# Latent attention block: queries in ten products with packed weights, partner rows by DMA, the split on GpSimd, another order

## The reference, cut to what matters

```python
q_hk  = (hidden_q @ Wq.T).reshape(B, S, 16, 128)
q_big = einsum('bshk,hkq->bshq', q_hk, w_kc_q)            # 192 wide, per head
q_big = q_big * cos_q + rotate_half(q_big) * sin_q        # partner of element j is j +- 96
kv_r  = rope(kv_c)                                        # 1601 keys, 64 wide
q_r   = einsum('bshq,hqr->bhsr', q_big, W_qr)
k_r   = einsum('bld,hdr->bhlr', kv_r, W_kr)
attn  = softmax(einsum('bhsr,bhlr->bhsl', q_r, k_r))
ctx_c = einsum('bhsl,bld->bhsd', attn, kv_r)
out   = einsum('bhsd,hkd->bhsk', ctx_c, w_kc_kv) ... @ Wo.T
```

## Time and profile before

| what | value |
|---|---|
| median of 3 runs | 1802.81 us (1801.43 to 1810.01) |
| profiled execution: its own time | 1803.73 us |
| profiled execution: span of instructions | 1802.5 us |
| busy over the span: PE, PEld, DVE, ACT, POOL | 93%, 82%, 80%, 67%, 45% |
| mean granted PE clock | 0.97 |
| chain that ended last | PE 72%, DVE 14%, ACT 4%, issue 4%, DMA 3%, POOL 2% |

### The profile page before, as it was taken

One profiled execution on the slowest core, in us unless ns is written; L12 is line 12 of the kernel. 1 busy time (PEld: TensorE's weight loads), 2 busy tenths in 40 slices (PEclk: granted clock), 3 DMA queues, 4 the chain that ended last, 5 costly groups with the idle time before them and its releaser, 6 DMA issues.

```text
span 1802.5 us, 40836 instructions
## 1 busy us (share of the span) xinstructions
PE 1673.0 (93%) x14656; PEld 1470.0 (82%) x14656; DVE 1439.6 (80%) x3666; ACT 1200.3 (67%) x3004; POOL 810.2 (45%) x720
## 2 busy tenths in 40 slices
PE   7999998889999888899999999999999998888995
PEld 6999976658866666799999999999999997665884
DVE  5777757859856865799999999999999997786995
ACT  5766764326634543688888888888888985542663
POOL 5744422247854532444434443444444441224774
PEclk8999999879999998899999999999999999998997
DMA  5000019332339000000000000000000002402233
GB/s 176 25 1 1 1 56 362 96 99 44 52 65 280 9 2 2 23 13 13 13 12 13 30 13 13 13 13 13 13 13 1 2 2 96 197 2 86 45 52 73
DMA packets 51860, 91.61 MB, mean 51 GB/s; under 512 B 4592, under 2 KB 43632, under 8 KB 49232
## 3 DMA queue, kind: packets, MB, share of 16 engines
q1 hardware_dynamic: 42928, 78.16, 13.0%
q0 software_dynamic: 8160, 10.29, 3.6%
q10 hardware_dynamic: 576, 0.56, 0.1%
HBM read 56.13 MB, written 32.87 MB: 49 GB/s over the span
## 4 chain that ended last, share of the span: by engine, by line
PE 72%; DVE 14%; ACT 4%; issue 4%; DMA 3%; POOL 2%; SPq 0%; DVEq 0%; ACTq 0%; POOLq 0%
PE bank L100 59%; PE bank L2680 10%; DVE a_t L707 1%; DVE d_nm L1442 1%; PE bank L1938 1%; DVE a_t L704 1%; DVE d_nm L1441 1%; DMA g_sums<-g_y,g_xs 1%; DMA c_sums<-c_y,c_xs 1%; POOL c_rows L1803 1%; PE bank L1910 1%; PE bank L505 1%; PE bank L1175 1%; DVE d_lifted L1470 1%; DVE tiny L133 0%
## 5 line engine op out<-in xcount | busy, mean ns | idle before, releaser
L2780 ACT ACTIVATE e_P<-bank,e_st 128x496 f32<-128x496 f32 (+2 forms) x512 | 305.8, 599 | 32.9 <-DVE e_st L2862 32.9
L2858 DVE TENSOR_REDUCE e_st<-bank 128x1 f32<-128x496 f32 (+2 forms) x512 | 288.4, 571 | 33.7 <-PE bank L100 23.7
L2881 DVE TENSOR_TENSOR e_PT_lo<-bank,e_PT_hi 128x512 fp32r<-128x512 f32 (+1 forms) x448 | 280.9, 644 | 30.3 <-ACT e_PT_hi L2800 29.3
L2680 PE MATMUL bank<-ident,e_P 128*128 128x128 f32 (+1 forms) x1664 | 256.6, 273 | 4.0 <-DVE e_PT_lo L2881 3.9
L2800 ACT CAST e_PT_hi<-bank 128x512 fp32r<-128x512 f32 (+1 forms) x448 | 247.0, 553 | 17.7 <-PE bank L2680 10.2
L100 PE MATMUL bank<-e_PT_hi,e_kv 128*128 128x256 f32 (+1 forms) x832 | 232.1, 300 | 3.1 <-DVE e_cx_lo L2888 3.1
L100 PE MATMUL bank<-e_PT_lo,e_kv 128*128 128x256 f32 (+1 forms) x832 | 214.8, 279 | 0.0
L100 PE MATMUL bank<-e_KT,e_qk_hi 128*128 128x496 f32 (+2 forms) x512 | 207.1, 405 | 5.2 <-ACT e_P L2780 3.8
L2680 PEld LDWEIGHTS bank<-ident,e_P 128*128 128x128 f32 (+1 forms) x1664 | 197.2, 140 | 17.5 <-issue 3.1
L100 PE MATMUL bank<-e_KT,e_qk_lo 128*128 128x496 f32 (+2 forms) x512 | 177.3, 346 | 0.0
L100 PEld LDWEIGHTS bank<-e_PT_hi,e_kv 128*128 128x128 f32 (+1 forms) x832 | 156.9, 189 | 8.5 <-DVE e_cx_lo L2888 3.8
(11 more groups left out here) (493 smaller groups left out, 5281.1 us busy)
## 6 DMA issues: line engine op xcount, KB each, us to landing
c_wall<-in_c_w SPq DMA_DIRECT2D x8, 1536.0 KB, 18.9
g_wall<-in_g_w SPq DMA_DIRECT2D x8, 1536.0 KB, 19.3
c_rows<-normed SPq DMA_DIRECT2D x9, 1040.0 KB, 12.0
g_rows<-normed SPq DMA_DIRECT2D x9, 1040.0 KB, 13.5
e_stage<-in_e_w SPq DMA_DIRECT2D x16, 416.0 KB, 3.2
c_xs<-c_rows SPq DMA_DIRECT2D x23, 130.0 KB
g_xs<-g_rows SPq DMA_DIRECT2D x23, 130.0 KB
landing<-in_a_wo SPq DMA_DIRECT2D x2, 1024.0 KB, 6.1
```

The lines of the kernel that those rows point to most:

```text
L2680: last = pe.transpose(o[0:rows, c * SEQ + i * P:c * SEQ + (i + 1) * P], p[:, i, k0:k0 + rows], ident[:])
L2780: act.activation(Pm[u % 2][:, i, STARTS[j]:STARTS[j] + n], bank[score_bank[j]][:, 0:n], ACT.Exp, bias=s[:, i, 4:5], accum_out=s[:, i, j:j ...
L2858: last = dve.tensor_reduce(s[:, i, j:j + 1], bank[score_bank[j]][:, 0:PIECES[j]], AX.X, ALU.max)
L2881: dve.tensor_tensor(lo, bank[tb_bank[at % 2]][0:rows, 0:n * SEQ].rearrange("p (c n) -> p c n", c=n), hi.bitcast(F32), ALU.subtract).then_i ...
```

## The change

- `project_q`: the folded weights of a head stand in one tensor of 384 columns: upper parts of 128 query rows, upper parts of the other 64, lower parts of those 64, lower parts of the 128. The first 128 rows take 2 chunks x 3 products as before. The other 64 rows take 2 chunks x 2 products: upper and lower weights side by side are one stationary matrix of 128 columns, multiplied by the upper and by the lower input. That makes 10 products. The rows that come from lower weights are carried as rows of their own through the rotation, and `w2` has the rows of the 64 twice, so that absorption (still 6 products, now of 128 rows) sums them.
- Query elements are reordered in groups of 32 so that the partner of a row is 32 partitions away: `swap` brings the partner rows to `r2` with four DMAs of 32 partitions on SP's queue for each unit; all tensors of the rotation have 128 partitions.
- `split_z` on POOL rounds and subtracts (the rounding was ACT's `upper_z`); one multiplication of 512 takes the place of two of 256 in `rope_q`. The rotation of unit 1 is issued before the block starts, `r1` and `r2` of odd units lie in a tensor that was there already.
- `lower_q` is two DVE instructions in place of one.
- The order of the steps in the loops of PE, ACT and DVE is another, the fetch of a head's weights is issued behind the swap of a unit, and the prefetch of block f is issued by ACT at the middle of the loop.

The diff, cut to its core (eight columns of indentation taken off):

```diff
                 ahead.sync_early()
+                ahead.sync_last()
 ...
                     routing.weigh(1)
-                if ahead and i == N:
-                    ahead.upper_z(0)
 ...
         self.kvb = [A(f"kv{b}", [P, KT, P], F32R) for b in range(BATCH)]
-        self.ropeq = A("ropeq", [HALFQ, 4, SEQ])
+        self.ropeq = A("ropeq", [P, 4, SEQ])
 ...
-        self.r1, self.r2 = ([x_in[0:HALFQ, 2 * i:2 * i + 2, :]] for i in range(2))
-        self.r0 = [x_in[0:HALFQ, 2 * i:2 * i + 2, :] for i in (2, 3)]
+        self.r1, self.r2 = ([x_in[:, 2 * i:2 * i + 2, :]] for i in range(2))
+        self.r0 = [x_in[:, 2 * i:2 * i + 2, :] for i in (2, 3)]
         flat = rows32[:, 1:TILES, :].rearrange("p a n -> p (a n)")
         self.swapped = [flat[:, i * n_ctx:(i + 1) * n_ctx].rearrange("p (k d) -> p k d", k=KT) for i in range(2)]
+        for n, x in enumerate((self.r1, self.r2)):
+            x.append(flat[:, 512 * n:512 * (n + 1)].rearrange("p (c n) -> p c n", c=2))
         self.ropek = landing[:, 0:2 * n_ctx].rearrange("p (a k d) -> p a k d", a=2, k=KT)
 ...
         self.k_turned, self.k_kept, self.padded = S_("k_turned"), S_("k_kept"), S_("padded")
+        self.q_swapped = [signal(f"xs_in{i}") for i in range(2)]
         self.twice = Count(sem("pool_link"))
 ...
-        QW, HALFQ = self.QW, self.HALFQ
+        QW = self.QW
         self.stage.append(A("stage", [P, 832]))
-        self.stage_r.append(A("stage_r", [LAT, 320]))
-        self.wq.append([A(f"wq_{x}", [P, DC, QW], F32R) for x in ("hi", "lo")])
-        self.w2.append([A(f"w2_{x}", [HALFQ, 2, P], F32R) for x in ("hi", "lo")])
-        self.qr.append([A(f"qr_{x}", [HALFQ, 2, SEQ], F32R) for x in ("hi", "lo")])
+        self.stage_r.append(A("stage_r", [LAT, 3 * P]))
+        self.wq.append(A("wq", [P, DC, 2 * QW], F32R))
+        self.w2.append([A(f"w2_{x}", [P, 2, P], F32R) for x in ("hi", "lo")])
+        self.qr.append([A(f"qr_{x}", [P, 2, SEQ], F32R) for x in ("hi", "lo")])
 ...
         sp.dma_start(self.stage_r[h % 2][:], t["e_wr"][h]).then_inc(*self.w_in[h % 2].up(16))
+
+    def swap(self, m):
+
+        sp.wait_ge(*self.q_kept.at(m + 1))
+        for q in range(4):
+            at, to = 32 * q, 32 * (q ^ 1)
+            sp.dma_start(self.r2[m % 2][to:to + 32], self.r0[m % 2][at:at + 32]).then_inc(*self.q_swapped[m % 2].up(16))
 ...
             sp.dma_start(self.ctx_raw[b % 2], t["ctx"][b]).then_inc(*self.ctx_in[b - 2].up(16))
+
+    def sync_last(self):
+        sp.wait_ge(*self.x_roped.at(BATCH))
+        for m in range(2):
+            self.swap(m)
 ...
     def fold_r(self, h, o):
-        r, QW, HALFQ = self.stage_r[h % 2], self.QW, self.HALFQ
+        r = self.stage_r[h % 2]
         for c in range(2):
-            last = mm(o[0:HALFQ, c * P:(c + 1) * P], r[:, c * HALFQ:(c + 1) * HALFQ], r[:, QW:QW + P], True, True)
+            last = mm(o[:, c * P:(c + 1) * P], r[:, c * P:(c + 1) * P], r[:, 2 * P:3 * P], True, True)
         last.then_inc(*self.r_folded.up())
 ...
         h, b = divmod(m, BATCH)
-        w, HALFQ = self.wq[h % 2], self.HALFQ
+        w = self.wq[h % 2]
         if m < BATCH:
 ...
         pe.wait_ge(*self.wq_lo.at(h + 1))
-        for c in range(2):
-            for d in range(DC):
-                last = mm3(o[0:HALFQ, c * SEQ:(c + 1) * SEQ], [x[:, d, c * HALFQ:(c + 1) * HALFQ] for x in w],
-                           (XT_hi[:, d, tok(b)], XT_lo[:, d, tok(b)]), d == 0, d == DC - 1)
+        for d in range(DC):
+            mm3(o[:, 0:SEQ], (w[:, d, 0:P], w[:, d, 2 * P:3 * P]), (XT_hi[:, d, tok(b)], XT_lo[:, d, tok(b)]),
+                d == 0, d == DC - 1)
+        for d in range(DC):
+            for n, x in enumerate((XT_hi, XT_lo)):
+                last = mm(o[:, SEQ:2 * SEQ], w[:, d, P:2 * P], x[:, d, tok(b)], d == 0 and n == 0,
+                          d == DC - 1 and n == 1)
         last.then_inc(*self.q_proj.up())
 ...
             act.wait_ge(*self.q_proj.at(BATCH * (h - 1)))
-        act.copy(self.wq[h % 2][0][:], o[:, 0:DC * self.QW].rearrange("p (c n) -> p c n", c=DC)).then_inc(*self.wq_hi.up())
+        act.copy(self.wq[h % 2][:, :, 0:self.QW], o[:, 0:DC * self.QW].rearrange("p (c n) -> p c n", c=DC)).then_inc(*self.wq_hi.up())
 ...
             act.wait_ge(*self.q_absorbed.at(BATCH * (h - 1)))
-        act.copy(self.w2[h % 2][0][:], o[0:self.HALFQ, 0:2 * P].rearrange("p (c n) -> p c n", c=2)).then_inc(*self.w2_hi.up())
+        act.copy(self.w2[h % 2][0][:], o[:, 0:2 * P].rearrange("p (c n) -> p c n", c=2)).then_inc(*self.w2_hi.up())
 ...
             act.wait_ge(*self.q_roped.at(m - 1))
-        act.copy(self.r0[m % 2].rearrange("p c n -> p (c n)"), o[0:self.HALFQ, :]).then_inc(*self.q_kept.up())
-
-    def upper_z(self, m):
-        act.wait_ge(*self.q_roped.at(m + 1))
-        if m >= 2:
-            act.wait_ge(*self.q_absorbed.at(m - 1))
-        act.copy(self.qr[m % 2][0][:], self.r1[m % 2]).then_inc(*self.z_hi.up())
+        act.copy(self.r0[m % 2].rearrange("p c n -> p (c n)"), o[:, :]).then_inc(*self.q_kept.up())
 ...
     def lower_q(self, h, o):
-        hi, lo = self.wq[h % 2]
+        w, src = self.wq[h % 2], o[:, 0:DC * self.QW].rearrange("p (c n) -> p c n", c=DC)
         dve.wait_ge(*self.wq_hi.at(h + 1))
-        dve.tensor_tensor(lo[:], o[:, 0:DC * self.QW].rearrange("p (c n) -> p c n", c=DC), hi[:].bitcast(F32),
-                          ALU.subtract).then_inc(*self.wq_lo.up())
+        for at, to in ((slice(0, P), slice(2 * P, 3 * P)), (slice(P, self.QW), slice(self.QW, 2 * P))):
+            last = dve.tensor_tensor(w[:, :, to], src[:, :, at], w[:, :, at].bitcast(F32), ALU.subtract)
+        last.then_inc(*self.wq_lo.up())
 ...
         dve.wait_ge(*self.w2_hi.at(h + 1))
-        dve.tensor_tensor(lo[:], o[0:self.HALFQ, 0:2 * P].rearrange("p (c n) -> p c n", c=2), hi[:].bitcast(F32),
+        dve.tensor_tensor(lo[:], o[:, 0:2 * P].rearrange("p (c n) -> p c n", c=2), hi[:].bitcast(F32),
                           ALU.subtract).then_inc(*self.w2_lo.up())
 ...
         pool.tensor_tensor(x1, v, self.ropeq[:, 0:2, :], ALU.mult)
-        for c in range(2):
-            last = pool.tensor_tensor(x2[:, c, :], v[:, 1 - c, :], self.ropeq[:, 2 + c, :], ALU.mult)
-        last.then_inc(self.twice.sem, 1)
+        pool.wait_ge(*self.q_swapped[m % 2].at(64 * (m // 2 + 1)))
+        pool.tensor_tensor(x2, x2, self.ropeq[:, 2:4, :], ALU.mult).then_inc(self.twice.sem, 1)
         pool.wait_ge(self.twice.sem, self.twice.step())
 ...
-    def lower_z(self, m):
+    def split_z(self, m):
         hi, lo = self.qr[m % 2]
+        pool.wait_ge(*self.q_roped.at(m + 1))
+        if m >= 2:
+            pool.wait_ge(*self.q_absorbed.at(m - 1))
+        pool.tensor_copy(hi[:], self.r1[m % 2]).then_inc(*self.z_hi.up())
         pool.wait_ge(*self.z_hi.at(m + 1))
 ...
         self.rope_q(0)
-        self.lower_z(0)
+        self.split_z(0)
+        self.rope_q(1)
 ...
 def latent_attention(latent, before, following):
-    H, HALFQ = 16, latent.HALFQ
+    H = 16
     LAG = 3
 ...
         latent.add_buffers(sc, 1)
-        for x, n in ((latent.r1, "r1"), (latent.r2, "r2")):
-            x.append(A(n, [HALFQ, 2, SEQ])[:])
         wf = latent.wf = [[A(f"wf{i}_{x}", [P, D], F32R) for x in ("hi", "lo")] for i in range(2)]
 ...
             sp.wait_ge(*before)
-            for h in range(1, H):
-                if h >= 2:
-                    sp.wait_ge(*latent.o_folded.at(h - 1))
-                latent.fetch(h)
-                if h == H // 2:
-                    prefetch(following)
+            latent.fetch(1)
+            for m in range(2, N):
+                latent.swap(m)
+                h, quarter = divmod(m, BATCH)
+                if h >= 1 and quarter == 0 and h + 1 < H:
+                    sp.wait_ge(*latent.o_folded.at(h))
+                    latent.fetch(h + 1)
 ...
                 u, v, w, after = a_unit(i), a_unit(i - 1), a_unit(i - 2), a_unit(i + 1)
                 h, quarter = i // BATCH + 1, i % BATCH
                 turn(v, 0)
+                attend(w, 4)
                 attend(w, 5)
-                score(u, 1, 0)
                 turn(v, 1)
                 attend(w, 6)
+                score(u, 1, 0)
+                project_q(a_unit(i + 2))
                 score(u, 1, 1)
-                absorb_q(after)
+                score(u, 1, 2)
                 turn(v, 2)
                 if i == N:
                     enter_tensor(0, enter_bank)
-                score(u, 1, 2)
+                score(u, 1, 3)
                 turn(v, 3)
-                score(u, 1, 3)
-                project_q(a_unit(i + 2))
+                absorb_q(after)
                 attend(v, 0)
+                attend(v, 1)
                 turn(v, 4)
-                attend(v, 1)
+                score(after, 0, 0)
+                attend(v, 2)
                 if h < H and quarter < 3:
                     (fold_q, fold_r, fold_o)[quarter](h)
-                score(after, 0, 0)
```

(65 more changed lines are left out.)

7 lines of the change are left out of this document (3 added, 4 removed).

## The result

| | before | after |
|---|---|---|
| median | 1803.68 us (1801.43 to 1810.01) | 1776.07 us (1772.51 to 1783.28, 4 runs) |
| ratio, 95% interval | | 0.9853 [0.9833, 0.9873] |
| profiled execution: time / span | 1803.73 / 1802.5 us | 1772.51 / 1771.3 us |
| busy for 785 to 1430 us: PE, DVE, ACT, POOL | 644.84, 585.80, 568.51, 280.02 | 645.00, 596.14, 554.79, 318.66 |

Before is here the median of four runs, made beside those of the changed kernel, 0.9 us above the one shown ahead. The kernel is faster by 27.6 us. The direction was right, the size was not.

The account below looks back on a forecast made before the run. It took PE, busy 664.40 of 664.56 us in the steady block, as the bound. Its terms, -14.3 + 0.5 + 0 - 0.6 - 0.7 = -15.1 us, took 1803.7 to 1788.6, named as 1788.0 us; range 1782 to 1798.

Parts of the forecast that it names:

- ten products for twelve: Query projection on PE: two products of 0.1175 us fewer in each of 61 units, 14.3 us saved, the main term.
- So PE is never kept waiting: Steady latent block: PE's only idle time is one 0.2 us wait, so each product issued or left out moves the end.
- The new order thus costs nothing: Reordered PE loop: all close meetings hold with little to spare; 0.5 us was taken for misses.
- The rounding moves ... nothing comes of it: Rounding from ACT to POOL: ACT gives up 0.62 us a unit but had 1.4 free, so no steady gain.
- 0.09 more for the product behind them: PE's loop: a product behind four transposes (0.35 us) costs 0.09 us more; the seven changes a unit stay.
- (a): Absorption on PE needs bank 7 read by ACT's keep_q, at 5.2 to 5.3 us; slack 0.3 us.
- (b): score(after, 0, 0) on PE needs DVE's lower_qk, ready at 7.4 us; slack 0.3 us.
- (c): The next absorption needs the split query after swap and POOL's instructions: 15.3 against 16.8 us, slack 1.5.
- The late chain: Rival: swap and five POOL instructions come late in every unit, costing the lateness x 61, about 1855 us; chance 0.05.
- (d): In units with fold_q, project_out needs lower_q, now two instructions; slack 0.2 us, each 0.1 missed costs 1.6 us.
- POOL on DVE: Rival: POOL's load, 0.43 to 0.57, slows DVE through shared ports; next to nothing expected; chance 0.01.
- I take 0.6 lost, so nothing net: Block entry: unit 0's longer rotation loses 0.6 us, against 0.65 us of projections in units 0 and 1.

Follow-up runs that it names:

- the repeat: The changed kernel measured once more, with nothing altered: 1779.25 us (4 runs), ratio 0.9872, 11.695 us a unit.
- the order alone: The kernel before with only the new order of the loops of PE, ACT and DVE: 1793.2 us, ratio 0.9943, 11.925 us a unit.
- old order: As a run: the changed kernel with the loops put back in their earlier order: 1917.43 us (one run), 13.877 us a unit.
- lengthened chain: The changed kernel with POOL's first multiplication done three times (2.7 us more), then five (5.4 us): 1795.11 and 1888.31 us.
- rounding on ACT: The changed kernel with the rounding back on ACT, behind upper_pt(v, 0) and ahead of exponential(u, 0, 0): 1807.64 us (10 runs), 12.124 us a unit.

## Why the prediction missed

**Right: ten products for twelve.** 14.3 us predicted, 14.1 measured by the units (0.228 x 62). The wider stationary tile costs nothing: the ten stand 0.118 us apart in the unit shown and 0.1166 in the mean, where the twelve of before had 0.1173. The rule on weight loads of the Trainium skill (TensorE: Matmul & The Clock Gate, "LDWEIGHTS (loading the stationary operand)"), taken as bare time in the stream, would have cost 16.5 us (estimate). The trace agrees with the rule on what the columns cost in the load itself: its records on PEld are 189 ns for 128 columns and 162 for 96, 27 apart as the 107 and 80 ns of the rule; but they run beside the products, and the distances show nothing of them.

**Wrong: "So PE is never kept waiting", and with it "The new order thus costs nothing".** This is the step that failed: the waits of the old order were put at nothing, and so was what a new order could gain. The earlier trace rows show 664.40 busy of 664.56 us, but a record of 0.28 us stands where the next start comes after 0.12, so a wait of up to 0.16 us leaves no idle time. The text had this ("The distance counts, not the record") and used it for prices only, never to ask whether each distance was as short as the rows of its kind allow. Before lost 0.11 us a unit in such waits, 0.09 of it at turn(v, 4) behind one chain through DVE. The new order removes them: -6.8 us in the steady part, where the sum had +0.5. The gain was larger than forecast by 12.5 us, of which this is 7.3; in the repeat (24.2 us) it is 7.3 of 9.1. The rest isn't assigned: the ends of the block and the untouched stages differ by up to 5 us between single executions, with the granted clock. (The sum itself has a slip of 0.3 us: 1788.6 less 0.9 is 1787.7, not 1788.0.)

**Right, with half a reason: "The rounding moves ... nothing comes of it".** In the old order even half of it away moved nothing (12.037 us a unit), and in the new order it cost nothing at the end of ACT's loop (the order alone). But at another place on ACT the same cast costs 0.43 us a unit. The prediction weighed ACT's total (1.4 us free) and not what stands behind the cast: the exponential that frees a bank for PE.

**Wrong, without effect: "0.09 more for the product behind them" as a cost of changing between transposes and products.** The sums come out right with it, since 0.35 and 0.09 are 4 x 0.109. As a price that fewer changes could save it doesn't exist.

**The meetings.** (a) 0.3 predicted, 0.22 measured; (b) 0.3 and 0.27. (c) 1.5 and 3.6 in the unit shown, 3.0 in the mean: the swap was taken at 4.7 us and comes at 3.9 behind keep_q, each of its DMAs is issued in 2.41 / 4 = 0.60 us and not 0.47, and the copy, taken at 1.3 us, takes 0.61. The late chain exists (old order, lengthened chain) and begins for single units before the mean slack is spent. (d) Missed by little: in units with fold_q the second product of project_out stands 0.16 us behind the first for 0.12, 15 x 0.04 = 0.6 us in all; with the order alone, where lower_q is still one instruction, it stands at 0.118. A unit without folds takes 11.18 us where 11.3 was predicted. The other rivals: DVE does not set the pace (596.14 of 645 us, a share of 0.92); the products are not longer.

**POOL on DVE.** L2881 of the earlier trace rows, now L2893, has a mean of 681 ns for its 128x512 form (683 in before) beside a POOL busy for 0.49 of the time (0.57 was predicted). With the chain lengthened by 2.7 us POOL was busy for 452.87 of 645 us, and DVE for 584.48, which is 10.80 us a unit as in after (596.14 x 11.699 / 645 = 10.81). The page of the Trainium skill on the shared ports (SBUF — State Buffer, "Who interferes with whom") names a lock, and exempts DVE instructions with at most one input in SBUF (outside their two-port modes, which a tensor_tensor doesn't have); L2893 is one, as its other input is a PSUM bank, and the trace agrees: no run here shows a cost.

**The ends.** At the entry the first score stood 15.81 us behind the last `d_q` and stands 15.73 behind it. That fits "I take 0.6 lost, so nothing net", but shows little: with the entry unchanged the same distance was 15.04 to 15.84 us in six other executions. Absorption(0) waited for the split query, its row and the instruction it waited for:

```profile
721.40 1.26 POOL L2542 TENSOR_TENSOR e_qr_lo<-x_in,e_qr_hi 128x512 fp32r<-128x512 f32 x1
...
722.76 0.36 PE L100 MATMUL bank<-e_qr_hi,e_w_hi 128*128 128x256 f32 x1 [1.97 <-issue]
```

1.97 us, over the bound of 1.4. The swap of unit 0 was usable 4.04 us behind keep_q. The fixed cost of 2.0 us that the prediction takes from the Trainium skill (DMA: Bandwidth & Descriptors, "Anatomy of one DMA — SWDGE (gpsimd) path") is that of DMAs issued by GpSimd; these are issued by SP, and with it the swap would have come at 3.6 us (estimate). Ahead of unit 1's scores, where ACT's rounding had stood in the way, PE's idle time fell from 2.05 us (at 735.55 in before) to 1.23 (at 730.28), 0.8 for 0.6 predicted, though PE was at the lower clock level there in after. From the last `e_qk_hi` to the last `e_cx_hi` the drain fell from 22.6 to 21.5 us, by 1.1 where 0.7 was predicted.

## What to carry over

A full engine in the profile can still be waiting: where records are longer than the distance between starts, list the mean distance for each kind of neighbours and look for the kind that is longer in one place than in another. A new order can then be priced as the waits it removes, not only as those it risks. For each instruction that moves to or from an engine, ask what stands right behind it there and who waits for that; the engine's free time in total doesn't answer it. To find what a hidden wait is for, measure from the end of each candidate: the one that counts stands at the same distance every time (0.147 us behind lower_pt, 0.142 behind the exponential). And a chain with a DMA in it must be measured in every unit and against its late landings, not in one unit or against its mean.

## What was not expected of the hardware

- Overlapping records of PE hid most of its waits (rounding on ACT): 4.3 us of idle time were shown for 23 us lost.
- A copy of 128x512 from float32 to fp32r took POOL 0.61 us, a two-input instruction of the same size 1.29 us.
- Four DMAs of 32 partitions (64 KB each, within SBUF) were issued in 2.41 us and usable 3.8 to 4.0 us after the source was ready in 43 of 55 units, 4.15 to 5.74 us in 12.
- A product starts 0.028 us behind a transpose where transposes stand 0.109 apart, and the next instruction comes 0.08 us later for it: changing between the two costs nothing.
- Within one kernel the time of an execution goes with PE's mean granted clock: 1.0 us for 0.001, over 66 executions of before.
